# Reciprocal row sums of an attention block spread over the partitions by a DMA through DRAM, instead of by a matmul

## The reference

```
x = x + attention(layernorm(x), ctx, ctx, k_length)        # q from x; keys and values are the context
x = x + moe(layernorm(x), Wg, w1, w2)

attention:  s    = SCALE * log(k_length)                   # one number for each batch
            attn = softmax(s * einsum('bhdq,bhdk->bhqk', q, k))
            out  = einsum('bhqk,bhdk->bhdq', attn, v)      # [b, h * d, q]
moe:        top 2 of 8 experts for each row of 512, capacity 1280, relu(x w1) w2, weighted sum
```

## Time and profile before

| what | value |
|---|---|
| timed runs | 2179.78, 2180.99, 2181.63 us, median 2180.99 |
| profiled execution, span from the first to the last instruction | 2177.8 us |
| share of the span: TensorE, VectorE, ScalarE, GpSimd | 97%, 46%, 33%, 22% |
| slots | from about 24 to 615 us, a period of 18.6 to 19.0 us in the steady part |
| tail of the attention part | to about 680 us |
| expert part | from about 680 us to the end |
| data moved | 216.61 MB, mean 99 GB/s |

### The profile page before, as it was taken

One profiled execution on the slowest core, in us unless ns is written; L12 is line 12 of the kernel. 1 busy time (PEld: TensorE's weight loads), 2 busy tenths in 40 slices (PEclk: granted clock), 3 DMA queues, 4 the chain that ended last, 5 costly groups with the idle time before them and its releaser, 6 DMA issues. The chain is left out here.

```text
span 2177.8 us, 27085 instructions
## 1 busy us (share of the span) xinstructions
PE 2117.0 (97%) x10179; PEld 1518.8 (70%) x10179; DVE 1008.1 (46%) x1908; ACT 712.9 (33%) x1216; POOL 470.4 (22%) x593
## 2 busy tenths in 40 slices
PE   3999999999999999999999999999999999999997
PEld 1445454455547888878888887888888788888776
DVE  5677878878765434234324423423432342343211
ACT  1666666666652222113212212311311231132110
POOL 3334444343422111110301201031030102101101
PEclk9999999999999999999999999999999999999999
DMA  9876767776635435212613612422441252241101
GB/s 147 160 165 157 181 157 188 168 187 162 146 114 161 115 70 132 58 22 85 131 20 78 150 26 58 125 50 43 114 98 25 56 134 52 48 125 31 16 6 20
DMA packets 183895, 216.61 MB, mean 99 GB/s; under 512 B 39731, under 2 KB 111419, under 8 KB 183740
## 3 DMA queue, kind: packets, MB, share of 16 engines
q1 hardware_dynamic: 154128, 173.21, 34.1%
q0 software_dynamic: 22240, 37.92, 9.1%
q10 hardware_dynamic: 7372, 3.42, 0.7%
HBM read 113.93 MB, written 68.29 MB: 84 GB/s over the span
## 5 line engine op out<-in xcount | busy, mean ns | idle before, releaser
L1590 DVE SCALAR_TENSOR_TENSOR hlo<-ps_h,hhi 128x512 fp32r<-128x512 f32 x256 | 177.0, 692 | 928.4 <-ACT hhi L1467 928.4
L1467 ACT ACTIVATE hhi<-ps_h 128x512 fp32r<-128x512 f32 x256 | 152.9, 597 | 1123.4 <-PE ps_h L1731 1123.4
L1729 PE MATMUL ps_h<-xhi,w1hi 128*128 128x512 f32 x1024 | 404.9, 395 | 2.5 <-PEq L1316 1.3
L1748 PE MATMUL ps_y<-w2hi,hhi 128*128 128x512 f32 x1024 | 404.7, 395 | 0.7 <-DVE hlo L1590 0.7
L1749 PE MATMUL ps_y<-w2lo,hhi 128*128 128x512 f32 x1024 | 403.0, 394 | 1.0 <-issue 1.0
L1750 PE MATMUL ps_y<-w2hi,hlo 128*128 128x512 f32 x1024 | 403.7, 394 | 0.0
L1731 PE MATMUL ps_h<-xhi,w1lo 128*128 128x512 f32 x1024 | 403.6, 394 | 0.0
L1730 PE MATMUL ps_h<-xlo,w1hi 128*128 128x512 f32 x1024 | 403.0, 394 | 0.0
L678 DVE TENSOR_REDUCE nmax<-ps_s 128x1 f32<-128x512 f32 x512 | 335.7, 681 | 128.5 <-PE ps_s L1086 124.6
L460 ACT ACTIVATE probs<-ps_t 128x512 f32<-128x512 f32 x504 | 273.0, 604 | 183.1 <-PE ps_t L1037 145.8
L1729 PEld LDWEIGHTS ps_h<-xhi,w1hi 128*128 128x128 f32 x1024 | 192.3, 188 | 48.5 <-issue 3.9
(11 more groups left out here) (202 smaller groups left out, 2007.2 us busy)
## 6 DMA issues: line engine op xcount, KB each, us to landing
raw<-in_L_ffn_w SPq DMA_DIRECT2D x128, 512.0 KB, 4.9
qst<-qhi SPq DMA_DIRECT2D x64, 256.0 KB, 5.8
xin<-dispatched SPq DMA_DIRECT2D x60, 256.0 KB, 5.8
kst<-khi SPq DMA_DIRECT2D x52, 256.0 KB, 6.4
xt<-in_x SPq DMA_DIRECT2D x32, 256.0 KB, 3.1
ct<-in_ctx SPq DMA_DIRECT2D x32, 256.0 KB, 4.5
qst<-qlo SPq DMA_DIRECT2D x32, 256.0 KB, 6.8
xres<-in_x SPq DMA_DIRECT2D x32, 256.0 KB, 4.7
```

Of the source, the lines that this page charges most:

```text
L1467: nc.scalar.activation(hhi[k % 2][:], ps_h[k % 3][:], ACT.Relu).then_inc(hhi_ready, 1)
L1590: nc.vector.scalar_tensor_tensor(hlo[k % 2][:], ps_h[k % 3][:], 0.0, hhi[k % 2][:].bitcast(F32), ALU.max, ALU.subtract).then_inc(h_ready, 1)
L1729: nc.tensor.matmul(to, w1hi[:, c, fs], xhi[n % 2][:, c, :], start=(c == 0), stop=False)
L1748: nc.tensor.matmul(ps_y[b][:], hhi[k % 2][:, bs], w2hi[:, f, :], start=(f == 0), stop=False)
```

## The change

The reciprocals go from `r_wide` [64, 32] (now two buffers) to a DRAM scratch of 4 x 512 by one DMA at (3, 0) of the slot s = g + 3, and from there by one DMA into `r_all` [128, 512], each head's row read 32 times, issued by ScalarE's queue at (0, 1) of the next slot. The multiply stands at (1, 3) of that slot instead of (1, 1). The split in a high and a low part, the matmul, its turn in the score ring, and `to_dims` with the instructions that make it are gone. GpSimd's residual waits for the multiply's own semaphore. In the tail, `weighed(G - 4)` takes the same way as the others.

```diff
-                if i == 1 and c == 1 and live(s - 4):
-                    s_turn["r", s - 4] = len(s_turn) + 1
...
+    shares = [nc.dram_tensor(f"shares{i}", (HPG, D), F32, kind="Internal").ap() for i in range(2)]
...
             def residual(g):
-                pool.wait_ge(s_free, s_turn["r", g])
+                pool.wait_ge(o_scaled, g + 1)
...
+            def shares_out(g):
+                act.wait_ge(r_ready, g + 1)
+                if g >= 2:
+                    act.wait_ge(r_ld[g % 2], 16 * turns(g - 2, 2))
+                act.dma_start(shares[g % 2].rearrange("h (c q) -> (h c) q", c=LW), r_wide[g % 2][:]
+                              ).then_inc(r_st[g % 2], 16)
+
+            def shares_in(g):
+                act.wait_ge(r_st[g % 2], 16 * turns(g, 2))
+                if g >= 2:
+                    act.wait_ge(o_scaled, g - 1)
+                act.dma_start(r_all[g % 2][:], shares[g % 2].unsqueeze(1).to_broadcast([HPG, HD, D])
+                              ).then_inc(r_ld[g % 2], 16)
...
                         if (c, i) == (3, 0) and live(s - 3):
-                            g = s - 3
-                            act.wait_ge(r_ready, g + 1)
-                            if g >= 2:
-                                act.wait_ge(s_done, s_turn["r", g - 2])
-                            for part in range(2):
-                                act.dma_start(r_rows[g % 2][HPG * part:HPG * part + HPG, :].bitcast(F32
-                                              ).rearrange("h (c q) -> h c q", c=LW),
-                                              r_hl[g % 2][:, part, :].bitcast(F32)).then_inc(r_ld[g % 2], 16)
+                            shares_out(s - 3)
+                        if (c, i) == (0, 1) and live(s - 4):
+                            shares_in(s - 4)
...
             for g in (G - 2, G - 1):
                 for c in range(NC4):
                     powers(g, c, 0)
+                    if g == G - 2 and c == 0:
+                        shares_in(G - 4)
...
+            def weighed(g):
+                if g <= G - 4:
+                    dve.wait_ge(r_ld[g % 2], 16 * turns(g, 2))
+                else:
+                    dve.wait_ge(l_saved, g + 1)
+                if g < G - 1:
+                    dve.wait_ge(o_saved, g + 1)
+                else:
+                    dve.wait_ge(pv_done, 4 * G)
+                    dve.wait_ge(x1_ready, g - 1)
+                nc.vector.tensor_tensor(o_sb[g % 2][:], (o_sb[g % 2] if g < G - 1 else ps_o)[:],
+                                        (r_all if g <= G - 4 else l_sb)[g % 2][:], ALU.mult).then_inc(o_scaled, 1)
...
                             dve.wait_ge(l_ld[g % 2], 16 * turns(g, 2))
-                            if g >= 1:
-                                dve.wait_ge(r_ready, g)
-                            nc.vector.reciprocal(r_wide[:], l_wide[g % 2][:]).then_inc(r_whole, 1)
-                            dve.wait_ge(r_whole, g + 1)
                             if g >= 2:
-                                dve.wait_ge(r_ld[g % 2], 32 * turns(g - 2, 2))
-                            nc.vector.tensor_copy(r_hl[g % 2][:, 0, :], r_wide[:]).then_inc(r_hi, 1)
-                            dve.wait_ge(r_hi, g + 1)
-                            nc.vector.tensor_tensor(r_hl[g % 2][:, 1, :], r_wide[:], r_hl[g % 2][:, 0, :].bitcast(F32),
-                                                    ALU.subtract).then_inc(r_ready, 1)
+                                dve.wait_ge(r_st[g % 2], 16 * turns(g - 2, 2))
+                            nc.vector.reciprocal(r_wide[g % 2][:], l_wide[g % 2][:]).then_inc(r_ready, 1)
...
-                        if (c, i) == (1, 1) and live(s - 4):
-                            g = s - 4
-                            k = s_turn["r", g]
-                            dve.wait_ge(s_done, k)
-                            dve.wait_ge(o_saved, g + 1)
-                            nc.vector.tensor_tensor(o_sb[g % 2][:], s_at(k)[:], o_sb[g % 2][:], ALU.mult
-                                                    ).then_inc(s_free, 1)
+                        if (c, i) == (1, 3) and live(s - 4):
+                            weighed(s - 4)
...
-            def shares(g):
-                pe.wait_ge(r_ld[g % 2], 32 * turns(g, 2))
-                if g == 0:
-                    pe.wait_ge(dims_st, 32)
-                bank = s_bank(s_turn["r", g])
-                nc.tensor.matmul(bank[:], to_dims[:], r_rows[g % 2][:], start=True, stop=True).then_inc(s_done, 1)
...
-                        if i == 1 and c == 1 and live(s - 4):
-                            shares(s - 4)
```

More of the change, by code:

```diff
@@ L97, in bank_turns @@
     t_turn["x2t", G - 1] = len(t_turn) + 1
-    for key in (("r", G - 4), ("logits", G - 5), ("places", B - 2), ("logits", G - 4), ("logits", G - 3),
+    for key in (("logits", G - 5), ("places", B - 2), ("logits", G - 4), ("logits", G - 3),
                 ("places", B - 1), ("logits", G - 2), ("places", B), ("logits", G - 1), ("places", B + 1), "total"):
@@ L155, in attention_and_dispatch @@
         l_wide = [sb(f"l_wide{i}", [HPG * LW, D // LW]) for i in range(2)]
[L156 to L160, removed]
+        r_wide = [sb(f"r_wide{i}", [HPG * LW, D // LW]) for i in range(2)]
+        r_all = [sb(f"r_all{i}", [P, D]) for i in range(2)]
         x1 = [sb(f"x1_{i}", [P, D]) for i in range(2)]
@@ L211, in attention_and_dispatch @@
         pv_done = sem("pv_done"); l_done = sem("l_done"); o_scaled = sem("o_scaled"); o_saved = sem("o_saved"); l_saved = sem("l_saved")
-        l_ld = sems("l_ld", 2); r_ld = sems("r_ld", 2)
-        r_whole = sem("r_whole"); r_hi = sem("r_hi"); r_ready = sem("r_ready")
-        dims_made = sem("dims_made"); dims_st = sem("dims_st"); x1_ready = sem("x1_ready")
+        l_ld = sems("l_ld", 2); r_st = sems("r_st", 2); r_ld = sems("r_ld", 2)
+        r_ready = sem("r_ready")
+        x1_ready = sem("x1_ready")
         stat2 = sem("stat2"); var2 = sem("var2"); veps2 = sem("veps2"); rstd2 = sem("rstd2")
@@ L379, in _ @@
             for s in range(-2, SLOTS):
[L380 to L386, removed]
                 if live(s + 2):
@@ L539, in _ @@
                         if g >= 2:
-                            act.wait_ge(r_whole, g - 1)
+                            act.wait_ge(r_ready, g - 1)
                         act.dma_start(l_wide[g % 2][:], l_sb[g % 2][0:P:HD, :].rearrange("h (c q) -> h c q", c=LW)
@@ L548, in _ @@
                         nc.scalar.activation(qhi[g % 2][:], qf[:], ACT.Copy).then_inc(qhi_ready, 1)
-                if s == 0:
-                    act.wait_ge(dims_made, 2)
-                    for part in range(2):
-                        act.dma_start(to_dims[HPG * part:HPG * part + HPG, :].bitcast(F32), dims[:]).then_inc(dims_st, 16)
                 if 1 <= s <= FILLS // 2:
@@ L809, in reciprocal @@
                 nc.vector.reciprocal(l_sb[g % 2][:], ps_l[:]).then_inc(l_saved, 1)
[L811 to L828 removed]
             def rows_added(g):
+                dve.wait_ge(o_scaled, g + 1)
                 dve.wait_ge(res_ld[g % 4], 16 * turns(g, 4))
@@ L1127, in _ @@
                     turned_logits(g, c, 1)
-                    if g == G - 2 and c == 0:
-                        shares(G - 4)
                     weighted(g if c else g - 1, (c - 1) % NC4)
```

18 lines of the change are left out of this document (removed).

## The result

| | before | after |
|---|---|---|
| median of the timed runs, us (4 each, side by side) | 2181.31 | 2237.30 |
| lowest to highest, us | 2179.78 to 2184.70 | 2231.36 to 2238.80 |
| ratio | | 1.0236, 95% from 1.0211 to 1.0261 |
| span of the profiled execution, us | 2177.8 | 2236.9 |
| last maximum of the attention part starts, us | 613.7 | 671.5 |

The kernel got slower by 56 us. The forecast was 2187 (2155 to 2207), so the measured time lies above its range. Nearly all of it is lost in the attention part: the last maximum starts 57.8 us later. From there to the first transposes of the expert part it is 4.0 us shorter, and from those to the end 5.3 longer: 57.8 - 4.0 + 5.3 = 59.1, the difference of the spans. I therefore read every experiment by the start of its last maximum.

A forecast was written before the change was run, and what follows sets the result against it. The attention part was taken as bound by TensorE's instruction stream, held up in places by the score banks that VectorE empties. 2177.8 - 27.7 - 0.4 + 34.4 = 2184.1 us, plus 3.2 for timed runs: 2187, range 2155 to 2207.

The forecast's parts named there:

- Nothing holds up the shorter run: the score matmul of (1, 3) then needs the maximum of (1, 0): Quarter 1 without the removed matmul: that maximum is done in time, so the full 0.99 us a slot is saved.
- the term of 27.7 us: Saving on TensorE from removing the matmul at (1, 1): 0.99 us in each of 28 slots.
- The lateness of the load: Load on four engines beside SP's copies lands 4.95 us behind the old matmul's place, late by 1.23 us a slot.
- Some 23.5 remain on these engines: at 0.077 each 1.8 us: Load's rows left when the copies end at 321.4: done in 1.8 us, landing at 323.8.
- some 1 to 2 us in most slots: Sign: VectorE's idle time ahead of the multiply at (1, 3), released by the load.
- The price of the wait: VectorE waiting at (1, 3) for the late load: 28 slots of 1.23 us, 34.4 us in all.
- rival c: The store lands late and ScalarE stands still at (0, 1): 2200 us or more, chance 0.04.
- under 4.8: Landing time in us of the 8 KB store of the shares, so ScalarE has no wait at (0, 1).
- VectorE's own work: The multiply moved to (1, 3) fits an idle gap: no cost with the load in time, otherwise 0.3 us a slot.
- TensorE's gaps ahead of later score matmuls: Sign: TensorE shows gaps ahead of the score matmuls of (2, 3) and (3, 3).
- the 1.47 us: Sign: quarter 1's first probabilities' matmul starts 1.47 us after the score matmul of (1, 1).
- Rival (d): Four engines never run empty, load late by over 2 us: 56 against 28.1 saved, 2209 us, chance 0.07.

The follow-up runs named there:

- e2: The changed kernel with only the first two groups' reciprocals loaded and reused by all others, the store kept; 2276.81 us, 1.0421 of before.
- e5: e2 with the row sums' DMA issued behind ScalarE's exponential of (1, 1); 2262.57 us, 1.0349 of before.
- e6: The kernel before with the row sums' DMA issued behind ScalarE's exponential of (1, 1); 2180.28 us, 0.9977 of before.
- e4: The changed kernel with the load issued by SP's queue ahead of the three q copies instead of by ScalarE; 2288.00 us, 1.0457 of before.
- e11: The changed kernel without SP's three copies into the q stack from group 5 on; 2278.94 us, 1.0439 of before.
- e1: The changed kernel, load kept, but the multiply takes the previous group's reciprocals, from three buffers; 2251.44 us, 1.0320 of before.
- e8: The changed kernel with the load issued at (1, 2), the multiply at (2, 3) and x1's statistics from (3, 2); 2198.60 us, 1.0059 of before.
- e9: e8 with the row sums' DMA issued behind ScalarE's exponential of (1, 1); 2173.61 us, 0.9963 of before.
- e3: The changed kernel with the load cut in four, one for each head, 32 partitions outermost; 2255.12 us, 1.0338 of before.

## Why the prediction was wrong

**The step that failed first** is "Nothing holds up the shorter run: the score matmul of (1, 3) then needs the maximum of (1, 0)". I followed one of the two rings of banks, that of the scores, and forgot the other: the turned logits of (1, 3) need the first exponential of quarter 1. It can be read in before's own timeline. ScalarE and its queue, then TensorE, in the first of the two slots:

```profile
299.67 0.59 ACT L537 ACTIVATE l_sb<-ps_l 128x512 f32<-128x512 f32 x1
300.29 0.58 ACTq L541 DMA_DIRECT2D l_wide<-l_sb  x1
300.97 2.07 ACT L460 ACTIVATE probs<-ps_t 128x512 f32<-128x512 f32 x4 [0.71 <-ACT l_sb L537]
```

```profile
299.04 0.50 PE L1086 MATMUL ps_s<-kst,qst 96*128 96x512 f32 x1
...
301.79 0.40 PE L1037 MATMUL ps_t<-qst,kst 98*128 98x512 f32 x1
```

In e2 the last turned matmul starts 304.25 - 303.60 = 0.65 us behind the start of those exponentials. By that it could start at 300.97 + 0.65 = 301.62 here, and it starts at 301.79: the saving to be had was 0.17 us a slot, not 0.99, or 4.8 us in 28. Over all 28 slots the mean from this exponential to this matmul is 0.77 us in before, so 3.5 us in all. Measured was no saving: e2, which leaves out the load as well, has its last maximum 1.9 us later than before (615.6 against 613.7), and its 28 slots are 0.5 us longer. Even with ScalarE's issue out of the way (e5) only 7.3 us of the 27.7 arrive (525.9 to 518.6), or 11.5 against the kernel before with the same edit (e6, 530.1). Without the term of 27.7 us the sum is 2215.

**The lateness of the load** was mis-sized. Its mechanism was right, four engines that share their time with the copies and VectorE waiting at the multiply: the scalar queue's packets rose to 9560; of these 8704 are the fills' 1280, 29 x 64 sums, 29 x 64 stores and 29 x 128 rows of the load, and the 856 others are 10 x 16 + 29 x 4 + 29 x 16 + 29 x 4, so of the sums, the store and the load one kind runs on sixteen engines and the other two on four. That the load is one of the two is shown by the 3828 packets that go with it in e4, and by the windows' share of 0.26 from 346 on. The Trainium skill ("DMA: Bandwidth & Descriptors", section "Rules for kernel authors") says that an outermost dimension below 16 confines a DMA to at most that many engines; both rows agree, with four. That the q copies slow it is shown by e11. But the landing came later: 10.8 and 9.4 us from issue to multiply in the slots shown, 9.75 in the median of the slots with a wait, where 8.7 was forecast, and at most 5.0 without the copies. One assumption was too kind. "Some 23.5 remain on these engines: at 0.077 each 1.8 us" had the rows right and their time wrong. From 346 on the four engines work alone until the multiply at 348.76, with GB/s of 57, 92 and 59, where four at 0.077 us a row would move 4 x 2048 B / 0.077 us = 106. That is about 194 KB, or 24 rows for each engine, in 2.8 us, so some 0.12 us a row (an estimate from the windows). VectorE's idle time was forecast at "some 1 to 2 us in most slots" and was 3.7 (99.3 / 27). The price of the wait was forecast at 34.4 us and measured at 50.5 (after against e1; 48.1 by the 28 slots), 1.80 a slot in place of 1.23.

**What the wait sets off.** I took the clock for constant. Added up over the windows of one us between 60 and 720, (1 - clock) x TensorE's busy time, after loses 13.6 us in 7 episodes (33 windows below 0.99, the first at 197, the last at 633), and e1, without the wait, 3.4. Before loses 6.7, all of it behind its last maximum. So up to some 10 of the 50.5 us may be the clock and not the wait itself. This is worked out from the windows; no run had the wait without the clock. It does not go with the length of the wait either: up to their last maxima e8 and e9 lose 13.5 and 13.1 us by the same sum, with waits for the load of 24.5 and 20.5 us in place of 99.3. What sets off their episodes is open.

**The store** (rival c) took a small part: ScalarE waits for it 11.6 us over 7 slots, and 7.8 over 5 in e1. Its median landing is 5.7 us, not "under 4.8", and just the 5.7 us that the prediction saw available. The tile view of the shares in after:

```profile
  ACT probs L449: 11.6, 7
...
DMA to landing us min/median/max: 1.7/5.7/7.6
```

**What held.** VectorE's own work cost nothing, while the load without a wait for it costs 5.4 us (e1 against e2; 8.2 by the 28 slots), which the sum had at nothing. The first of these is argued from e2, which has VectorE's new order and is not slower than before; no run tested it alone. Of the signs that the prediction named, VectorE's idle time ahead of the multiply and TensorE's gaps ahead of later score matmuls came, and the 1.47 us did not. From before to after in the attention part: +1.9 for the matmul and all else that went, +5.4 for the traffic, +50.5 for the wait, 57.8 in all; by the 28 slots +0.5, +8.2 and +48.1, 56.8 in all. The two small terms are not clear of what single profiles can differ by: the profile of e6 is 4.2 us longer than before's by the 28 slots, while its median is 4.5 shorter. Rival (d), late by over 2 us at 2209, named what happened to the load best, and still credited 28 us of saving that did not exist.

## What to carry to other kernels

Before a removed operation is credited, follow every ring of buffers through the stretch, not only that of the fullest engine: here TensorE was 99.62% busy, and ScalarE's two saves and its DMA issue held the quarter from which a matmul was taken. Price a DMA that something will wait for by what runs on the DMA engines at its time and by how many of them it uses, and put its issue where they are idle; a place at the head of a queue did not do it here. And look at the granted clock behind a new wait that stops TensorE, for the wait can cost more than its length where the clock falls.

## What the runs showed of the hardware

In kernels in which VectorE waits for the load in most slots, the granted clock falls in episodes. The stretch of 130 to 600 us in e4_load_first:

```profile
130.00:600.00 470.00, 414.20 (x2341) 198.21 (x2344) 296.90 (x743) 251.24 (x469) 160.33 (x250) 0.92 0.78 151
```

Its clock is 0.92, where after has 0.98 and before 1.00; by the same sum e4 loses 45.4 us of clock in 18 episodes, and e3 27.4 in 13. That may be a good part of why these two attempts ended worse than after (13.6): their last maxima come 52.2 and 4.2 us later than its own. No run separates the clock from the waits.

An 8 KB store to DRAM lands in 1.7 us at the least, 5.7 in the median and 7.6 at the most in the same kernel; what sets it no run isolates. The same 256 KB load takes at most 5.0 us from issue to use without the q copies (e11) and 9.4 to 10.8 beside copies between SBUF and SBUF (after). The Trainium skill ("DMA: Bandwidth & Descriptors", section "Issuing engines are not separate DMA queues") says that DMAs interleave on the 16 engines whoever issues them; these numbers agree. An issue on ScalarE's queue took 0.31 to 1.64 us where four stood in a row (e3), and 0.55 where one did.
